# A fused attention and state-space kernel: merged products, a mask added by VectorE, setup inside the loop, and a scan on half-width weights

## The reference

```
U = (layernorm(x) @ W_in.T + b_in) @ Bmat            # 64 columns a step
s = silu(s @ A.T) + u_t     for t in 0..127          # the scan, over all 128 batches
out = x + states @ Cmat + (mean(program_probs) @ W_prog.T + b_prog)
```

## Time and profile before

| | |
|---|---|
| median of 3 runs | 4208.76 us (4208.7 to 4211.23) |
| the profiled execution | 4207.95 us, of which the span is 4206.2 |
| PE, DVE, ACT, POOL busy | 96%, 82%, 76%, 69% of the span |
| mean granted clock of TensorE | 0.989 |
| DMA | 38 GB/s in the mean |
| chain that ended last | PE 67%, ACT 12%, POOL 7%, issue 5%, DVE 4% |
| first 20 us and last 110 us | DMA share 0.89 and some 0.7, in between 0.1 |

### The profile page before, as it was taken

The page is one execution under the profiler, slowest core; times in us unless marked ns, Lnnn a source line. Parts: engine busy times, 40 slices in busy tenths (PEclk is TensorE's granted clock), DMA queues, the critical chain, the costliest instruction groups (busy, mean ns, idle before and its releaser), DMA issues.

```text
span 4206.2 us, 112214 instructions
## 1 busy us (share of the span) xinstructions
PE 4042.6 (96%) x37547; PEld 3383.5 (80%) x37547; DVE 3431.2 (82%) x9517; ACT 3175.7 (76%) x6733; POOL 2911.0 (69%) x3172
## 2 busy tenths in 40 slices
PE   4899999999999999999999999999999999999859
PEld 3688888888888888888888888888888888888645
DVE  3688888888888888888888888888888888888634
ACT  1577887887788778877887787788778877887632
POOL 0477777777777777777777777777777777777634
PEclk9999999999999999999999999999999999999979
DMA  3000100010001100000100010101000000100037
GB/s 108 19 25 25 33 30 28 25 33 30 28 25 33 30 28 26 30 29 27 31 30 28 25 33 30 28 25 33 30 28 26 30 28 25 33 30 25 17 103 272
DMA packets 116547, 159.98 MB, mean 38 GB/s; under 512 B 11350, under 2 KB 103323, under 8 KB 111579
## 3 DMA queue, kind: packets, MB, share of 16 engines
q1 hardware_dynamic: 111626, 146.75, 11.2%
q10 hardware_dynamic: 4368, 6.17, 0.5%
HBM read 115.01 MB, written 37.88 MB: 36 GB/s over the span
## 4 chain that ended last, share of the span: by engine, by line
PE 67%; ACT 12%; POOL 7%; issue 5%; DVE 4%; DMA 0%; ACTq 0%; DVEq 0%; POOLq 0%; SPq 0%
PE bank L674 15%; PE bank L744 9%; PE bank L666 7%; PE bank L682 6%; PE bank L858 4%; PE bank L714 3%; ACT prob L992 3%; PE bank L778 3%; PE bank L693 3%; PE bank L773 2%; POOL rs_ln L1404 2%; PE bank L791 2%; POOL X L1424 2%; POOL X L1418 2%; ACT probT L1002 2%
## 5 line engine op out<-in xcount | busy, mean ns | idle before, releaser
L1158 DVE TENSOR_REDUCE mx<-bank 128x4 f32<-128x512 f32 x1280 | 837.6, 681 | 90.4 <-PE bank L714 68.6
L1169 DVE TENSOR_TENSOR prob<-bank,mx 128x512 f32<-128x512 f32 x1280 | 847.8, 679 | 54.6 <-PE bank L744 33.8
L1002 ACT ACTIVATE probT<-bank 128x512 f32<-128x512 f32 x1280 | 753.3, 600 | 158.9 <-PE bank L778 100.5
L992 ACT ACTIVATE prob<-prob 128x512 f32<-128x512 f32 x1280 | 795.6, 641 | 22.0 <-DVE prob L1169 20.9
L982 ACT ACTIVATE turned<-bank 128x512 f32<-128x512 f32 x896 | 531.9, 616 | 344.0 <-PE bank L666 223.5
L744 PE MATMUL bank<-ident,prob 128*128 128x128 f32 x5120 | 746.3, 277 | 20.3 <-DVE den L1180 6.5
L744 PEld LDWEIGHTS bank<-ident,prob 128*128 128x128 f32 x5120 | 591.3, 142 | 124.9 <-issue 36.8
L674 PE MATMUL bank<-turned,shared 128*128 128x256 f32 x2560 | 605.7, 384 | 1.8 <-ACT turned L982 1.8
L674 PEld LDWEIGHTS bank<-turned,shared 128*128 128x128 f32 x2560 | 468.3, 191 | 69.9 <-issue 14.3
L1404 POOL TENSOR_TENSOR rs_ln<-ve_ln,half 128x2 f32<-128x2 f32 x320 | 226.4, 707 | 384.9 <-DVE ve_ln L1147 384.9
L1483 POOL TENSOR_SCALAR shared<-turned,half_of 128x512 f32<-128x512 f32 x256 | 399.1, 1570 | 79.9 <-ACT turned L982 79.9
(11 more groups left out here) (242 smaller groups left out, 9047.8 us busy)
## 6 DMA issues: line engine op xcount, KB each, us to landing
shared<-in_x SPq DMA_DIRECT2D x128, 256.0 KB, 3.0
CB<-in_ctx SPq DMA_DIRECT2D x64, 256.0 KB, 3.4
CC<-in_ctx SPq DMA_DIRECT2D x64, 256.0 KB, 2.8
mod<-mod_rows SPq DMA_DIRECT2D x64, 256.0 KB, 3.3
residual<-X SPq DMA_DIRECT2D x64, 256.0 KB, 3.5
out<-turned SPq DMA_DIRECT2D x16, 1024.0 KB, 4.8
turned<-residual SPq DMA_DIRECT2D x14, 1024.0 KB, 7.3
u_turned<-us SPq DMA_DIRECT2D x64, 64.0 KB, 2.4
```

Source lines behind the costliest of these rows:

```text
L992: nc.scalar.activation(flat(t), flat(t), ACT.Exp, scale=SCALE[p]).then_inc(*st["act"].mark(f"exp.{b}{r}"))
L1002: nc.scalar.activation(flat(t), banks.of(f"{att}.turn.{b}{r}")[:, :], ACT.Copy).then_inc(*st["act"].mark(f"probT.{b}{r}"))
L1158: nc.vector.tensor_reduce(m[:], banks.of(f"{att}.tile.{b}{r}")[:, :].rearrange("p (h t) -> p h t", h=4), AX, ALU.max)\
L1169: nc.vector.tensor_tensor(t[:], banks.of(f"{att}.tile.{b}{r}")[:, :].rearrange("p (h t) -> p h t", h=4), maxes.of(f"{att}.max.{b}{r}")[:]. ...
```

## The change

- **Mask.** The eight `causal` products of a group are gone. DVE adds the mask while it moves a tile of `self_att` from its bank to `prob` (`mask`), takes the maximum from there (`max`), and ACT subtracts it as a bias in the exponential, which therefore is four instructions of 128 columns for a tile instead of one of 512. The factor of the scores goes into the weights of `q1`. The `ctx` and `mix` tiles stay as they are.
- **Gate.** `vx` is gone: its 4 columns are appended to the weights of `mix_in.v`, which now writes 260 columns into each of two banks. The probabilities are normalized by DVE before they are turned (`part1`), `av1` gives its result turned (weights of 4 columns), ACT does gelu with the bias, and `yT` and its copy are gone. `cross` has weights of 32 rows, in two row quarters and two banks.
- **u.** `mix_out.u` has weights of 64 columns, one batch in each half of the columns.
- **Setup.** Only 7 loads stand ahead of the loop. The others are issued by SP ahead of bodies 1 and 2 and by ACT ahead of body 2; the folding and the mean are done ahead of body 3 (`prepare`), by all engines in the same order as before, and each engine's list goes on behind it.
- **Scan.** The product with `a_two` has weights of 64 columns; the output product is two products of 64 batches, in the two halves of the columns.
- **Lists.** `PROGRAM` and `BANKS` are new for all engines. SP's loop is written out like the others.

The diff, cut to its core (of the lists only PE's is shown):

```diff
     "pe": """
-        mix_att.scores.00@6 ctx_att.turn.12@4 ctx_att.values.01@4 ctx_att.values.03@4 ctx_att.values.00@4
-        ctx_att.values.02@4 pair.yT@5 ctx_att.turn.10@4 ctx_att.turn.11@4 pair.cross@5 self_att.causal.02@2
-        ctx_in.x1T@3 real.ccT@5 ctx_att.turn.13@4 mix_in.k@5 ctx_att.back.0@4 self_att.causal.00@2
-        ctx_att.values.10@4 ctx_att.values.13@4 ctx_att.values.12@4 ctx_att.values.11@4 self_att.causal.03@2
-        self_att.causal.01@2 self_att.scores.01@2 self_att.scores.03@2 self_att.scores.02@2 self_att.scores.00@2
-        mix_att.turn.03@6 ctx_att.back.1@4 ctx_in.q@3 mix_att.turn.02@6 pair.ncT@5 self_in.len@2 mix_att.turn.00@6
-        self_in.xT@1 pair.sc2@5 self_att.causal.11@2 self_att.causal.10@2 self_att.causal.12@2 mix_att.turn.01@6
-        self_att.scores.10@2 self_att.scores.12@2 self_att.scores.11@2 mix_att.values.00@6 mix_att.values.02@6
-        mix_att.values.01@6 mix_att.values.03@6 pair.pT2@5 self_att.turn.01@2 ctx_in.cT@3 pair.av@5 mix_in.v@5
-        self_att.turn.00@2 ffn.x2T@4 ctx_in.k@3 ffn.fc1@4 real.x4T@5 ctx_in.e0@3 self_att.turn.03@2
-        self_att.causal.13@2 real.screal@5 ffn.fc2@4 mix_out.o@6 real.pTreal@5 self_att.turn.12@2 self_att.turn.02@2
-        real.av@5 ctx_in.len@3 self_att.scores.13@2 ctx_att.scores.03@3 ctx_att.scores.00@3 ctx_att.scores.01@3
-        ctx_att.scores.02@3 self_att.values.00@2 self_att.values.02@2 self_att.values.03@2 self_att.values.01@2
-        self_in.q@1 self_att.turn.11@2 self_att.turn.10@2 ctx_in.v@3 self_att.turn.13@2 self_att.back.0@2
-        self_in.v@1 ctx_att.turn.00@3 ctx_att.turn.01@3 self_att.values.12@2 self_att.values.13@2
-        self_att.values.10@2 self_att.values.11@2 ctx_att.scores.10@3 ctx_att.scores.13@3 ctx_att.scores.11@3
-        ctx_att.scores.12@3 pair.CT@4 self_in.k@1 mix_out.h6T@6 pair.FT@4 ctx_att.turn.03@3 real.h5T@5
-        self_att.back.1@2 pair.sc1@4 mix_in.q@5 ctx_att.turn.02@3 pair.vx@4 pair.pT1@4 mix_out.u@6 pair.av1@4
-        self_in.e0@1
+        self_in.e0@2 ctx_att.values.01@4 mix_att.scores.00@6 pair.cross@5 ctx_att.turn.12@4 ctx_att.values.03@4
+        ctx_att.turn.11@4 ctx_att.values.02@4 ctx_att.values.00@4 ctx_att.turn.10@4 mix_in.k@5 ctx_att.turn.13@4
+        ctx_att.back.0@4 ctx_in.x1T@3 ctx_att.values.10@4 ctx_att.values.12@4 ctx_att.values.11@4
+        ctx_att.values.13@4 self_att.scores.01@2 self_att.scores.00@2 ctx_att.back.1@4 ctx_in.cT@3 ctx_in.q@3
+        pair.ncT@5 real.ccT@5 mix_att.turn.02@6 pair.sc2@5 mix_att.turn.00@6 ctx_in.k@3 mix_att.turn.03@6 pair.pT2@5
+        self_att.scores.02@2 self_att.scores.11@2 self_att.scores.10@2 self_att.scores.03@2 pair.av@5
+        mix_att.turn.01@6 mix_att.values.00@6 mix_att.values.02@6 mix_att.values.03@6 self_att.turn.01@2 ffn.x2T@4
+        mix_att.values.01@6 self_in.len@2 self_in.xT@1 ffn.fc1@4 ctx_in.e0@3 self_att.turn.00@2 real.x4T@5 ffn.fc2@4
+        real.screal@5 self_att.turn.02@2 mix_out.o@6 self_att.scores.13@2 self_att.scores.12@2 ctx_att.scores.01@3
+        self_att.turn.03@2 self_att.turn.10@2 real.pTreal@5 self_att.values.02@2 self_att.values.00@2
+        self_att.values.01@2 self_att.values.03@2 real.av@5 self_in.k@1 self_in.q@1 self_att.turn.11@2 mix_out.h6T@6
+        ctx_att.scores.03@3 ctx_att.scores.00@3 ctx_att.scores.02@3 self_att.turn.13@2 self_att.turn.12@2
+        self_att.back.0@2 ctx_att.turn.01@3 ctx_in.v@3 pair.CT@4 self_att.values.10@2 self_att.values.12@2
+        self_att.values.13@2 self_att.values.11@2 self_in.v@1 ctx_att.scores.13@3 ctx_att.scores.12@3
+        ctx_att.scores.11@3 ctx_att.turn.03@3 ctx_in.len@3 real.h5T@5 pair.FT@4 self_att.back.1@2 mix_in.v@4
+        pair.sc1@4 ctx_att.turn.02@3 mix_out.u@6 ctx_att.turn.00@3 mix_in.q@5 pair.pT1@4 ctx_att.scores.10@3
+        pair.av1@4
...
+PREPARED, MOD_STORED = 3, 5
+PREP_BANKS = (0, 2, 4)
...
-                def causal_(b, r):
-                        nc.tensor.matmul(t[:, :], ident_b[:], causal[:].rearrange("p h t -> p (h t)"), start=True, stop=False,
-                                         skip_group_check=True).then_inc(*self_att["pe"].mark(f"causal.{b}{r}"))
...
+                        t, free = banks.claim(f"{att}.tile.{b}{r}", u_att["dve"], f"{SHIFTS[p]}.{b}{r}")
...
-                def vx(g):
-                    t, free = banks.claim("pair.vx", pair["act"], "vx")
-                    for w in latest(free, pair["dve"].done("NXT", g)):
+                def v3(g):
+                    took = [banks.claim(f"mix_in.v{b}", mix_in["act"], "v") for b in range(G)]
+                    for w in latest(*(free for _, free in took)):
                         pe.wait_ge(*w)
-                    for b in range(G):
+                    for w in latest(pair["act"].done("HCT", g)):
+                        pe.wait_ge(*w)
+                    for b, (t, _) in enumerate(took):
                         for a in range(DH):
-                            last = nc.tensor.matmul(t[:, b * 4:b * 4 + 4], trn["NXT"][:, a, b * S:(b + 1) * S],
-                                                    w_gate[:, a, :], start=(a == 0), stop=(a == DH - 1))
-                    last.then_inc(*pair["pe"].mark("vx"))
+                            last = nc.tensor.matmul(t[:, 0:D + 4], trn["HCT"][:, a, b * S:(b + 1) * S], w_v3[:, a, :],
+                                                    start=(a == 0), stop=(a == DH - 1))
+                    last.then_inc(*mix_in["pe"].mark("v"))
...
-                        last = nc.tensor.matmul(t[:, b * 4:b * 4 + 4], pct["1"][:, b, :], vxs[:, b, :], start=True, stop=True)
+                        last = nc.tensor.matmul(t[32 * b:32 * b + 4, 0:S], vp3[g % 2][:, b, D:D + 4], pct["1"][:, b, :], start=True, stop=True)
...
-                        last = nc.tensor.matmul(t[:, b * D:(b + 1) * D], y5T[:, b, :], w_cross[:], start=True, stop=True)
+                    for b, (t, _) in enumerate(took):
+                        rows_ = slice(32 * b, 32 * b + 32)
+                        last = nc.tensor.matmul(t[:, 0:D], y5T[rows_, :], w_cross[rows_, :], start=True, stop=True)
...
-                        last = nc.tensor.matmul(t[:, 0:W], w_u[:, a, :], trn["H6T"][:, a, :], start=(a == 0), stop=(a == DH - 1))
+                        for b in range(G):
+                            last = nc.tensor.matmul(t[NS * b:NS * b + NS, 0:S], w_u[:, a, :], trn["H6T"][:, a, b * S:(b + 1) * S],
+                                                    start=(a == 0), stop=(a == DH - 1))
...
+                def masked(b, r):
+                    att, st = "self_att", self_att
+                    def mask_(g):
+                        t, free = probs.claim(f"{att}.mask.{b}{r}", st["pe"], f"turn.{b}{r}")
+                        for w in latest(free, st["pe"].done(f"scores.{b}{r}", g)):
+                            dve.wait_ge(*w)
+                        nc.vector.tensor_tensor(t[:], banks.of(f"{att}.tile.{b}{r}")[:, :].rearrange("p (h t) -> p h t", h=4),
+                                                causal[:].unsqueeze(1).to_broadcast([128, 4, 128]), ALU.add).then_inc(*st["dve"].mark(f"mask.{b}{r}"))
+                    def low(g):
+                        m, free = maxes.claim(f"{att}.max.{b}{r}", st["act"], f"exp.{b}{r}")
+                        for w in latest(free, st["dve"].done(f"mask.{b}{r}", g)):
+                            dve.wait_ge(*w)
+                        nc.vector.tensor_reduce(m[:], probs.of(f"{att}.mask.{b}{r}")[:], AX, ALU.max, negate=True)\
+                            .then_inc(*st["dve"].mark(f"max.{b}{r}"))
+                    return {f"mask.{b}{r}": mask_, f"max.{b}{r}": low}
...
+                    def masked(g):
+                        for w in latest(st["dve"].done(f"max.{b}{r}", g)):
+                            act.wait_ge(*w)
+                        low = maxes.of(f"{att}.max.{b}{r}")
+                        for h in range(4):
+                            last = nc.scalar.activation(t[:, h, :], t[:, h, :], ACT.Exp, bias=low[:, h:h + 1], scale=1.0)
+                        last.then_inc(*st["act"].mark(f"exp.{b}{r}"))
+                    return masked if p == "self" else centred
...
-                def a4r(g):
-                    for w in latest(pair["dve"].done("rs1", g), pair["pe"].done("av1", g), pair["act"].before("gelu", g)):
+                def part1(g):
+                    for w in latest(pair["dve"].done("rs1", g)):
                         dve.wait_ge(*w)
-                    nc.vector.tensor_tensor(a4[:], banks.of("pair.av1")[:, 0:G * 4].rearrange("p (b c) -> p b c", b=G),
-                                            rsum["1"][:].unsqueeze(2).to_broadcast([128, G, 4]), ALU.mult)\
-                        .then_inc(*pair["dve"].mark("a4r"))
-                def a4_(g):
-                    for w in latest(pair["dve"].done("a4r", g)):
-                        dve.wait_ge(*w)
-                    nc.vector.tensor_tensor(a4[:], a4[:], gate_b[:].unsqueeze(1).to_broadcast([128, G, 4]), ALU.add)\
```

(47 more changed lines are left out.)

616 lines of the change are left out of this document (290 added, 326 removed).

## The result

The change takes 23 us, not 105: 4185.39 us median of five runs (4181.85 to 4188.11) against 4208.76 (4208.23 to 4211.23, five runs), a ratio of 0.9942 [0.9930, 0.9955]. The forecast of 4104 and its range up to 4175 were wrong; the sign was right. The profiled execution of after took 4181.85 us, its span is 4180.1. From here on "a group" is the median distance of one step of PE (`e0` of `ctx_in`) over the 64 groups: 60.59 us before, 60.83 after.

What follows compares the result with a forecast made beforehand. TensorE (PE) bounds the loop at 60.59 us a group, falling to 59.6 with waits. From 4208 us, −64 for the loop, −33 for setup and −7 for the scan gave 4104 us; range 4035 to 4175, likeliest 4060 to 4145.

Steps and rivals of the forecast that it cites:

- the sign: The whole kernel: the change makes it faster, chance 0.90.
- e0: PE step on column quarters, 8 rows of 128 columns in 0.36 us; by its rate av1 was to save 0.21.
- Products removed or narrowed: PE's work in one group: causal, vx and yT gone, av1, cross and u cheaper, together −3.9 us.
- Score runs and changes of form: PE's new list, per group: six score runs for five, +0.86 us; 31 switches between full and quarter products for 20, +1.87.
- The rival that had these changes nearly free: PE's list: switching between full and quarter products costs almost nothing, group 57.7 us, time 3982; chance 0.14 (3960 to 4060).
- ACT, DVE and POOL: Other engines' work per group: ACT rises to 53.9 us (52.6 to 56.2), DVE stays at 52.3, POOL at 44.5.
- Waits: PE's idle time per group: 0.2 us now, 0.2 (0 to 1) added, giving a period of 59.6.
- The third rival: ACT's in-order queue takes over and the kernel is slower: 8.5 us of waits give period 62.4, time 4284; chance 0.07.
- Setup: Before and early in the loop: first turn at 12 us, −52, less a stop of about 19; net −33 us (−22 to −42).
- Scan: The scan's chain: a narrower first weight load saves 0.055 us a step, −7 us.

Runs made afterwards that it cites:

- after_no_gelu: The changed kernel with Identity in place of gelu, so that both table loads of a group go: 4091.13 us, ratio 0.9721.
- after_one_exp: The changed kernel with one 512-column exponential per self_att tile, the first head's maximum as bias for all four heads: 4178.74 us, ratio 0.9929.
- before_four_changes: The kernel before with two turn steps put between ctx_att's values steps, four changes of form more and no other work: 4367.39 us, ratio 1.0378.

## Why the prediction failed

- **Products removed or narrowed: right.** Forecast −3.9. By distances between starts, means over forty groups: `causal` −1.93 (its 0.1 of change of form included), `vx` −0.81, `yT` −0.33, `av1` and `e0` together −0.41, `cross` −0.24, `u` −0.28. The last two gained less and the others more: −4.0.
- **Score runs and changes of form: right in sum.** Forecast +0.86 +1.87 = +2.7. The score rows (L571) take 6.47 instead of 5.52, +0.95: a run of 4, 8, 12 or 16 rows takes 1.05, 1.07, 1.08 or 1.10, so each run more costs the same, however short it is. PE's sum went from 60.6 to 59.3 with −4.0 of products, so by difference all that was added is +2.7. (The counts of 20 and 31 changes take the scores and values of `mix`, L731 and L773 before, as products on row and column quarters, which they are; the section on the kernel before calls all other products full.) The rival that had these changes nearly free (3982) is out: after_no_gelu has nothing else in PE's way and stands at 59.33.
- **ACT, DVE and POOL: right** to 1.1 us: 54.5, 51.2, 43.8.
- **Waits: wrong, and this is the miss.** "PE has 0.2 us of idle a group now; I add 0.2 (0 to 1)". That makes 0.4, and it was 1.6. The term was guessed from PE's idle time before, which only says that the old lists were well covered. What was not done is to walk through the new lists and lay the chain of each engine beside the work of PE between its two ends. For the gelu that could be done from the new lists and the trace of before: its two table loads, 1.28 each, and PE's rows for the steps that the new list has between `av1` and `turn.10`. The change takes `yT` and its copy out of the chain, but it also brings `cross` nearer to `av1` (4.75 us of PE's work between them, now 1.9) and puts `ctx_att.exp.10` behind the second table load, so that 5.8 us of ACT stand against 4.8 of PE. So 60.83 came instead of 59.6: 1.2 us, 78 us over the 63 distances.
- **The third rival was half right.** It said that a period over 60.5, with PE idle before ACT's rows, would come if ACT's waits stay when work is added. The sign came; the reason did not. ACT's waits fell from 11.8 to 6.4 us a group, near the 5.5 of slack that the forecast had, and under the 7.4 from which on the rival was to decide. Its load was not it (after_one_exp); one chain through it was.
- **Setup: right in sum, by errors that cancel.** −33 forecast, −33.4 measured. First turn 9.6 instead of 12, but a stop of 28 us for late loads and `prepare` instead of 19. Of the 54.6 us of earlier start 21 were lost again by the first `e0` of `ctx_in`, 7 less than the stop; where the 7 were hidden was not followed up.
- **Scan: right.** −7 forecast, −8.3 (−4 to −12) alone on the kernel before, −5.5 from the last group to the end here.

The loop was to give −64 and gave +13; the other two terms were met to 2 us.

The prediction drew on the Trainium skill, TensorEngine Tiling (Array Packing), Tiling Modes, for the rule that a change of the tiling mode drains the engine. The runs agree in that each change has a price, 0.13 to 0.20 us in before_four_changes; the draining itself is not seen in them. By the speed-ups in the same page's Overview alone, the prediction's estimate was a period of 57.7. The 59.33 of after_no_gelu, in a list that goes back and forth 31 times a group, speaks against that.

## What to carry to other kernels

When a change rewrites the order of work, the bound engine's sum is only half of the forecast. Take each chain that leaves that engine and comes back (through a table load, a copy, a maximum), add up its durations, and beside it what the engine's new list holds between the two ends; the difference is the wait, and both sides can be read from rows of the kernel before. This gives the wait at the place one looks at, and no more: the four orders that moved `exp.10` did end the wait of `turn.10` on it, and their forecasts of the time still missed by 100 to 210 us. In these lists, which keep PE at 97%, none of the six reorderings tried was free: each moved step was somebody's cover, held somebody's bank, or fed somebody's chain. So name all three before moving a step, and look at the granted clock behind every new wait.
